# Splitting expert weights on GpSimd instead of ScalarE and VectorE in a perceiver, attention and experts kernel

## The reference, cut to what matters

```python
# x: (8, 64, 512), ctx: (8, 1601, 512), all float32
x = x + xattn(layernorm(x), ctx, ...)    # 3 rounds of slot attention with a GRU cell
x = x + attn(layernorm(x), Wqkv, bqkv, Wo, bo)   # 16 heads of 32, sequences of 64
x = x + ffn(layernorm(x), ...)

def _expert(xf, w1, w3, w2):
    return jax.nn.silu(xf @ w1) * (xf @ w3) @ w2

def ffn(x, ...):                         # 512 rows in all, D = 512, H = 256
    logits = xf @ router_w + router_b
    topk_vals, topk_idx = jax.lax.top_k(logits, 2)
    gates = softmax over the two chosen experts, 0 for the others
    routed = jax.vmap(_expert, in_axes=(None, 0, 0, 0))(xf, routed_w1, routed_w3, routed_w2)   # 8 experts
    routed_out = jnp.einsum('etd,te->td', routed, gates)
    shared_out = the same with 2 shared experts, summed
    return routed_out + shared_out
```

## Time and profile before

| what | us |
|---|---|
| median of 3 runs | 975.69 (975.63 to 976.13) |
| the profiled execution | 976.91 |
| its span in the trace | 975.2 |
| `head_attention`, from POOL's memset to its last DVE instruction | 734.99 to 813.68 |
| POOL's constants in `experts`, L1613 to L1618 | 813.96 to 815.11 |
| `experts`, shared blocks and what lies ahead of them | 813.96 to 886.03 |
| `experts`, routed blocks | 886.03 to about 953.6 |

### The profile page before, as it was taken

The page is one execution under the profiler, slowest core; times in us unless marked ns, Lnnn a source line. Parts: engine busy times, 40 slices in busy tenths (PEclk is TensorE's granted clock), DMA queues, the critical chain, the costliest instruction groups (busy, mean ns, idle before and its releaser), DMA issues. The chain is left out here.

```text
span 975.2 us, 37746 instructions
## 1 busy us (share of the span) xinstructions
PE 789.1 (81%) x17278; PEld 657.8 (67%) x17278; DVE 594.9 (61%) x1109; ACT 366.1 (38%) x714; POOL 145.8 (15%) x390
## 2 busy tenths in 40 slices
PE   3697789989889979889989797956797866786991
PEld 1445689889889979789979797856456644333440
DVE  2777456866776947857857746353425765895222
ACT  3676415324424315434335212011235523573330
POOL 3020111211313021304113111010000000130003
PEclk9799789999999999999999999987796985887996
DMA  9867970372380480843451806033349305041435
GB/s 343 320 131 133 242 144 5 52 148 96 64 228 5 68 224 4 139 154 53 58 186 31 197 4 132 5 114 103 121 87 300 100 20 180 18 130 33 128 89 161
DMA packets 178953, 115.74 MB, mean 119 GB/s; under 512 B 145196, under 2 KB 157540, under 8 KB 175596
## 3 DMA queue, kind: packets, MB, share of 16 engines
q1 hardware_dynamic: 166048, 100.45, 41.2%
q10 hardware_dynamic: 11004, 7.61, 2.6%
q0 software_dynamic: 1744, 5.27, 1.9%
HBM read 61.94 MB, written 12.85 MB: 77 GB/s over the span
## 5 line engine op out<-in xcount | busy, mean ns | idle before, releaser
L987 PE MATMUL score<-qa,ctxT 128*128 128x64 f16 x3744 | 122.6, 196 | 19.3 <-issue 11.6
L987 PEld LDWEIGHTS score<-qa,ctxT 128*128 128x128 f16 x3744 | 118.7, 100 | 21.7 <-issue 13.0
L1006 PE MATMUL score<-qa,unit 128*128 128x64 f16 (+1 forms) x2496 | 122.8, 197 | 9.9 <-issue 8.2
L1006 PEld LDWEIGHTS score<-qa,unit 128*128 128x128 f16 (+1 forms) x2496 | 121.4, 101 | 11.5 <-issue 11.3
L1006 PE MATMUL score<-scratch,unit 128*128 128x64 f16 (+1 forms) x1248 | 121.1, 197 | 3.1 <-issue 3.1
L938 PEld LDWEIGHTS gate<-hs,whhT 128*128 128x128 f16 x3456 | 112.3, 100 | 16.7 <-issue 10.7
L938 PE MATMUL gate<-hs,whhT 128*128 128x64 f16 x3456 | 114.6, 196 | 9.7 <-issue 9.2
L1006 PEld LDWEIGHTS score<-scratch,unit 128*128 128x128 f16 (+1 forms) x1248 | 114.9, 101 | 2.8 <-issue 2.8
L938 PE MATMUL gate<-qa,Bt 128*128 128x64 f16 x3456 | 105.2, 193 | 3.2 <-DVE qa L761 2.8
L938 PEld LDWEIGHTS gate<-qa,Bt 128*128 128x128 f16 x3456 | 102.6, 98 | 3.6 <-DVE qa L761 3.0
L516 ACT ACTIVATE unit<-unit,rrow 128x512 f16<-128x512 f32 x96 | 65.4, 716 | 34.3 <-POOL rrow L95 18.9
(11 more groups left out here) (254 smaller groups left out, 1343.7 us busy)
## 6 DMA issues: line engine op xcount, KB each, us to landing
unit<-in_ctx_dram SPq DMA_DIRECT2D x23, 1024.0 KB, 9.8
wall<-in_L_ffn_routed_w_dram SPq DMA_DIRECT2D x24, 512.0 KB, 8.7
xg_scratch<-wall SPq DMA_DIRECT2D x1, 3840.0 KB, 15.0
y_scratch<-ctxT ACTq DMA_DIRECT2D x15, 256.0 KB, 2.0
ctxT<-in_L_xattn_gru_wih_dram SPq DMA_DIRECT2D x3, 1024.0 KB, 17.5
ctxT<-in_L_xattn_gru_whh_dram SPq DMA_DIRECT2D x1, 3072.0 KB, 26.0
ctxT<-in_L_attn_Wqkv_dram SPq DMA_DIRECT2D x12, 256.0 KB, 8.3
ctxT<-in_L_ffn_shared_w_dram SPq DMA_DIRECT2D x6, 512.0 KB, 6.2
```

Of the source, the lines that this page charges most:

```text
L987: mm = pe.matmul(score[n][:, t * K:(t + 1) * K], a, q, start=(k == 0), stop=(k == 3 * DC - 1), skip_group_check=True)
L1006: mm = pe.matmul(score[n][:, dc * K:(dc + 1) * K], a, q, start=first, stop=True, skip_group_check=True)
```

## The change

POOL takes over the split of all 12 shared pieces and of 26 (`BY_POOL`) of the 48 routed ones. [...] The 12 shared pieces and routed pieces 0 to 13 (`IN_HEADS`) are done in `head_attention` behind the memset, routed pieces 14 to 25 in `experts` between the constants and the scatter. ACT and DVE keep pieces 26 to 47, 22 in all, spread as 2, 3, 3, 3, 2, 3, 3, 3 over the shared blocks, and lose the four big instructions for the shared weights. ACT's first piece, 26, waits until POOL has done 25 pieces, its second until it has done 26; both waits stand in ACT's list behind `tanh_of(0)`. The shared halves now lie in place in `ctxT`, so `got`, `ysb` and `gs` move to `e.room`, and two waits on the shared split go.

```diff
+BY_POOL = 26
+IN_HEADS = 14
@@ head_attention, gpsimd
             pool.memset(prob, 0.0).then_inc(zeroed, 1)
+            for n in range(NS * CHUNKS):
+                if n % CHUNKS == 0:
+                    pool.wait_ge(e_all.shared_in[n // CHUNKS], 48)
+                if n >= 2:
+                    pool.wait_ge(e_all.shared_split, n - 1)
+                split_on(pool, e_all, "shared", n, n, e_all.shared_split)
+            routed_on(pool, e_all, 0, IN_HEADS)
@@
+def halves_of(e, kind, n):
+
+    if kind == "routed":
+        span, high, low = e.wall[:], 2 * n, 2 * n + 3
+        raw = span[:, low:low + 2]
+    else:
+        span, high, low = e.free[1].bitcast(F16).rearrange("p (s d) -> p s d", d=D), max(2 * n - 1, 0), 2 * n + 2
+        raw = span[:, low:low + 2]
+    return raw.rearrange("p s d -> p (s d)").bitcast(F32), span[:, high], span[:, low]
+
+def split_on(pool, e, kind, n, count, done):
+
+    raw, high, low = halves_of(e, kind, n)
+    pool.tensor_scalar(raw, raw, WS, None, ALU.mult).then_inc(e.scaled, 1)
+    pool.wait_ge(e.scaled, count + 1)
+    pool.tensor_copy(high, raw).then_inc(e.high_made, 1)
+    pool.wait_ge(e.high_made, count + 1)
+    pool.tensor_tensor(low, raw, high, ALU.subtract).then_inc(done, 1)
+
+def routed_on(pool, e, first, end):
+
+    for n in range(first, end):
+        if n % CHUNKS == 0:
+            pool.wait_ge(e.wall_in[n // CHUNKS], 48)
+        if n >= 2:
+            pool.wait_ge(e.routed_split, n - 1)
+        split_on(pool, e, "routed", n, NS * CHUNKS + n, e.routed_split)
@@ experts
-        ws = e.room[:, 0:NS * CHUNKS * D].bitcast(F16).rearrange("p (n i c d) -> p n i c d", n=NS, i=2, c=CHUNKS)
-        got = in_1[:, 0:2 * RT * D].rearrange("p (j t d) -> p j t d", j=2, t=RT)
-        ysb = in_1[:, 2 * RT * D:3 * RT * D].rearrange("p (b d) -> p b d", b=RT)
+        got = e.room[:, 0:2 * RT * D].rearrange("p (j t d) -> p j t d", j=2, t=RT)
+        ysb = e.room[:, 2 * RT * D:3 * RT * D].rearrange("p (b d) -> p b d", b=RT)
@@
         def chunks_in(b):
-            return (min(CHUNKS * b, NW), min(CHUNKS * (b + 1), NW))
+            n = NW - BY_POOL
+            return (BY_POOL + n * b // NSB, BY_POOL + n * (b + 1) // NSB) if b < NSB else (NW, NW)
@@ experts, gpsimd
+            routed_on(pool, e, IN_HEADS, BY_POOL)
             pool.wait_ge(e.zeroed, 16)
...
-            pool.wait_ge(ws_lo, NS)
-            pool.wait_ge(ws_hi, NS)
@@ experts, scalar: shared_high(0) ahead of the router and shared_high(1) at b = 1 go
                 for n in range(first, end):
-                    if n % CHUNKS == 0:
+                    if n % CHUNKS == 0 or n == BY_POOL:
                         act.wait_ge(wall_in[n // CHUNKS], 48)
-                    if n >= 2:
-                        act.wait_ge(wall_lo, n - 1)
-                    act.activation(wall[:, 2 * n], wall_raw(n), ACT.Copy, scale=WS).then_inc(wall_hi, 1)
+                    if n < BY_POOL + 2:
+                        act.wait_ge(e.routed_split, n - 1)
+                    else:
+                        act.wait_ge(wall_lo, n - 1 - BY_POOL)
+                    raw, high, low = halves_of(e, "routed", n)
+                    act.activation(high, raw, ACT.Copy, scale=WS).then_inc(wall_hi, 1)
@@ experts, vector: shared_low(0) behind normalise and shared_low(1) behind find_places go
@@ experts, tensor
-                    pe.wait_ge(ws_hi, s + 1)
-                    pe.wait_ge(ws_lo, s + 1)
+                    if t == 0:
+                        pe.wait_ge(e.shared_split, CHUNKS * (s + 1))
                 else:
                     if k == 0:
-                        pe.wait_ge(wall_hi, NW)
-                        pe.wait_ge(wall_lo, NW)
+                        pe.wait_ge(e.routed_split, BY_POOL)
+                        pe.wait_ge(wall_hi, NW - BY_POOL)
+                        pe.wait_ge(wall_lo, NW - BY_POOL)
```

More of the change, by code:

```diff
@@ L1544, in experts @@
         th = in_0[:, 3 * RT * D:].rearrange("p (b h) -> p b h", b=2)
-        gs = in_1[:, 3 * RT * D:].bitcast(F16).rearrange("p (b i h r) -> p b i h r", b=2, i=2, h=HH)
-        spare = e.room[:, NS * CHUNKS * D:]
+        spare = e.room[:, 3 * RT * D:]
+        gs = spare[:, D:2 * D].bitcast(F16).rearrange("p (b i h r) -> p b i h r", b=2, i=2, h=HH)
         earlier = spare[:, 0:P]
@@ L1566, in experts @@
         x_ready, x_turned, x_out, x_hi, x_lo, r_in, x16_hi, x16_lo, routed, consts, picked, counted, gexp_in, gexp_out, gates_out, \
-            placed, owned, scattered, ws_hi, ws_lo, wall_hi, wall_lo, hid_done, tanhd, g_done, g_turned, gs_hi, gs_lo, \
+            placed, owned, scattered, wall_hi, wall_lo, hid_done, tanhd, g_done, g_turned, gs_hi, gs_lo, \
             down_done, shared_out, y_copied, summed, o_out, dve_done = (sem(n) for n in (
                 "x_ready", "x_turned", "x_out", "x_hi", "x_lo", "r_in", "x16_hi", "x16_lo", "routed", "consts", "picked", "counted",
-                "gexp_in", "gexp_out", "gates_out", "placed", "owned", "scattered", "ws_hi", "ws_lo", "wall_hi", "wall_lo",
+                "gexp_in", "gexp_out", "gates_out", "placed", "owned", "scattered", "wall_hi", "wall_lo",
                 "hid_done", "tanhd", "g_done", "g_turned", "gs_hi", "gs_lo", "down_done", "shared_out", "y_copied", "summed", "o_out",
@@ L1586, in wall_half, with shared_half @@
             return span[:, bass.ds(reg, 1), 2 * chunk].rearrange("p a d -> p (a d)")
+        def shared_half(s, i, chunk):
+            return halves_of(e, "shared", CHUNKS * s + chunk)[1 + i]
         def chunks_in(b):
-            return (min(CHUNKS * b, NW), min(CHUNKS * (b + 1), NW))
+            n = NW - BY_POOL
+            return (BY_POOL + n * b // NSB, BY_POOL + n * (b + 1) // NSB) if b < NSB else (NW, NW)
         block = ctx.enter_context(nc.Block())
@@ L1638, in _ @@
         def _(act):
-            def shared_high(s):
-                act.wait_ge(e.shared_in[s], 48)
-                act.activation(ws[:, s, 0].rearrange("p c d -> p (c d)"), shared_raw[s], ACT.Copy, scale=WS).then_inc(ws_hi, 1)
             def wall_high(first, end):
                 for n in range(first, end):
-                    if n % CHUNKS == 0:
+                    if n % CHUNKS == 0 or n == BY_POOL:
                         act.wait_ge(wall_in[n // CHUNKS], 48)
-                    if n >= 2:
-                        act.wait_ge(wall_lo, n - 1)
-                    act.activation(wall[:, 2 * n], wall_raw(n), ACT.Copy, scale=WS).then_inc(wall_hi, 1)
+                    if n < BY_POOL + 2:
[4 more added lines that the diff above has]
+                    act.activation(high, raw, ACT.Copy, scale=WS).then_inc(wall_hi, 1)
             def tanh_of(b):
@@ L1697, in _ @@
             st = Steps(dve, dve_done)
[L1699 to L1702, removed]
             def wall_low(first, end):
                 for n in range(first, end):
-                    dve.wait_ge(wall_hi, n + 1)
-                    dve.scalar_tensor_tensor(wall[:, 2 * n + 3], wall_raw(n), WS, wall[:, 2 * n], ALU.mult, ALU.subtract).then_inc(wall_lo, 1)
+                    dve.wait_ge(wall_hi, n + 1 - BY_POOL)
+                    raw, high, low = halves_of(e, "routed", n)
+                    dve.scalar_tensor_tensor(low, raw, WS, high, ALU.mult, ALU.subtract).then_inc(wall_lo, 1)
             def gated(b):
@@ L1786, in _ @@
             normalise(dve, st, rows, xn, e.mv, small, x_ready)
-            shared_low(0)
             dve.wait_ge(x_hi, 1)
@@ L1795, in _ @@
                     find_places()
-                    shared_low(1)
                 if b == 4:
@@ L1839, in w_half @@
                     def w_half(i):
-                        return ws[:, s, i, dc] if k < 0 else wall_half(owner_of[k], i, dc)
+                        return shared_half(s, i, dc) if k < 0 else wall_half(owner_of[k], i, dc)
                     for a, w in split_passes(x_half, w_half):
@@ L1865, in w_half @@
                     def w_half(i):
-                        return ws[:, s, i, DC + h] if k < 0 else wall_half(owner_of[k], i, DC + h)
+                        return shared_half(s, i, DC + h) if k < 0 else wall_half(owner_of[k], i, DC + h)
                     for a, w in split_passes(lambda i: gs[:, b % 2, i, h], w_half):
@@ L1946, in perceiver_kernel @@
         e.free = (words(big.ctxT[0]), words(big.ctxT[1]), in_last[:, RT * D:])
-        e.raw = [e.free[1][:, n * CHUNKS * D:(n + 1) * CHUNKS * D] for n in range(NS)]
+        e.raw = [e.free[1][:, (n * CHUNKS + 1) * D:((n + 1) * CHUNKS + 1) * D] for n in range(NS)]
         e.xg_d = nc.dram_tensor("xg_scratch", [NB * P, 2 * D], F16)
@@ L1958, in perceiver_kernel @@
         e.wall_in = [sem(f"wall_in{n}") for n in range(NE)]
+        e.scaled, e.high_made = sem("scaled"), sem("high_made")
+        e.shared_split, e.routed_split = sem("shared_split"), sem("routed_split")
         big.v_moved = sem("v_moved")
```

8 lines of the change are left out of this document (removed).

## The result

The changed kernel took 998.12 us in the median of 4 runs (996.5 to 1000.64), the kernel before 975.66 in 4 runs beside it (971.88 to 976.13). The ratio is 1.0241, with a 95% interval of 1.0207 to 1.0275. The forecast was 994.4, slower, with a range of 966 to 1006.

The account below looks back on a forecast made before the run. DVE was taken to bound the shared stage. The head stage's +16.3 and +2.4 up to the first routed block gave +18.7 us: 995.6 by the profiled execution, 994.4 us for the median, range 966 to 1006.

Parts of the forecast that it names:

- The price of a piece: POOL's multiplication, copy, subtraction and waits for one piece: 3.43 us, bounds 2.48 and 4.22.
- The head stage: In `head_attention`, POOL's 26 pieces plus 4 us lost beside DVE end the stage later: +16.3 us.
- Two of the signs: POOL's last head-stage piece some 16 us after DVE's last instruction; ACT waiting 15 to 20 us ahead of pieces 26 and 27.
- The second tanh: In `experts`, `tanh_of(1)` waits in ACT's list for POOL and starts at H + 44.2, before H + 26.8; H is the stage's start.
- 1 beside DVE: In `experts` ahead of `tanh_of(1)`, POOL loses 1 us beside DVE during its 12 pieces.
- From there to block 8: From `tanh_of(1)` to the first routed block: 32.7 us, before 45.3.
- The clock of block 8: At the first routed block, PE's first 12 matmuls run at full clock, 2.59 us and not 5.04: 2.4 less.
- The moved buffers and the removed waits: In `experts`, the other buffer for `got` and `ysb` costs nothing, and the removed waits had long been met.
- Rival 1: POOL's multiplication runs at L94's rate, a piece is 2.57 us, the head stage's end stays: -8.0 us, 967.7; 28%.
- Rival 2: Pieces are quick, but DVE's L1393 pairs wait for POOL: +5.6 in the head stage, -2.2 behind, +3.4, 979.1; 20%.
- The crossing: The whole change's effect crosses zero at about 3.1 us a piece; below 2.95 the head-stage term is gone.

Follow-up runs that it names:

- e1: The changed kernel with POOL's multiplication written with two operations (multiply, add 0.0) in place of one; 979.97 us, ratio 1.0027.
- e4: The changed kernel with only the 12 shared pieces on POOL, in the head stage, and all 48 routed pieces on ACT and DVE; 975.80 us, ratio 0.9985.
- e7: e1 with the sums of the exponentials kept in PSUM and not in SBUF; 974.72 us, ratio 0.9988 to the kernel before.
- e6: The changed kernel with only the shared pieces on POOL, moved to the projections, plus 80 POOL memsets in the head stage; 976.02 us, one execution.
- e8: e7 with the shared pieces on POOL in the projections and all 26 routed ones in the head stage; 965.52 us, ratio 0.9895.

## Why the prediction was right, step by step

- **The price of a piece: right.** 3.43 forecast, 3.37 measured undisturbed. The disputed term, the multiplication in the form of L90, went L90's way, and e1 shows that it is the form: with two operations it took 0.62, near the 0.53 that L94 gave. The 0.77 us estimated from the Trainium skill, GPSIMD Engine Reference, section 3.1 (Elementwise, side-by-side cycle accounting), fit neither this instruction (1.49) nor the copy (0.61); the measurement decides.
- **The head stage: right, +16.3 forecast, +17.4 measured.** POOL lost 6.7 us beside DVE (94.3 us for 26 pieces of 3.37) and not 4. Two of the signs came out otherwise: POOL's last piece ended 6.7 us after DVE's last instruction and not some 16, since DVE's own stage had grown by 10.7, for which the forecast had no term; and ACT waited 26.2 us ahead of pieces 26 and 27 (23.5 and 2.7), not 15 to 20. The sum was right for this kernel because POOL's stage, the longer one, hid DVE's.
- **The second tanh: mis-sized by 2.7 us.** H + 44.2 forecast, 46.9 measured. The term "1 beside DVE" in `experts` was the fault: two instructions of 2.29 us with two inputs cost POOL 2.0 and 2.1 us, 45.0 for the 12 pieces in place of 42.2.
- **From there to block 8: 32.7 forecast, 30.2 measured.** The term that was too long is the 7.3 us from `gated(2)` to the turn at 861.35, which I kept from the kernel before: here it was 4.6 (885.83 to 890.45). The difference goes with PE's clock. Before, PE had stood idle for 6.1 us ahead of this work and had a granted clock of 0.50 from 854.5 to 857.6; here it had stood for 1.0 us, and the clock was 1.00 from 886.3 to 890.6. The same two groups of matmuls, before and after:

```profile
855.02 2.77 PE L1869 MATMUL e_y<-room,ctxT 128*128 128x512 f16 x6
857.58 3.93 PE L1843 MATMUL e_hid<-room,unit 128*128 128x512 f16 x12
```

```profile
886.56 1.46 PE L1896 MATMUL e_y<-ctxT,room 128*128 128x512 f16 x6
887.86 2.75 PE L1870 MATMUL e_hid<-ctxT,unit 128*128 128x512 f16 x12
```

The last block's work took 4.6 us (902.96 to 907.53) where I had 4.4. That this error nearly cancels the one before it is luck.

- **The clock of block 8: wrong here.** I took 2.4 us off, since PE's pause would be 3 us. The pause was 3.10, and the first 12 matmuls still took 5.30, at a granted clock of 0.50 in 907.5 to 911.0, the lower of its two levels (1.2 and not 2.4 GHz). In e1, with a pause of 3.09, they ran at the full one (the rest stage is 86.94); in e7, with 3.09 too, they took 5.30 again. A pause of 3 us doesn't settle it; what does is open. This term makes most of the 3 us between 18.7 forecast and 21.9 measured in the spans.
- **The moved buffers and the removed waits: nothing,** as forecast (e4: 0.35 us).
- **Rival 1 (quick pieces, 967.7) was wrong in its second half.** e1 made the pieces quick, and the time was 979.97.
- **Rival 2 (quick pieces, DVE pays, 979.1) described e1,** its total even to 1 us, but by two errors of opposite sign. In the head stage it had +5.6 and +10.7 came: its term for the 16 instructions was right (5.3), but the other eight, which it left out, grew by 4.0, and 1.4 came on top, with a granted clock of 0.72 against 0.79. Behind the stage it had -2.2, with the clock in it, and -7.0 came: -4.8 up to block 8 and -2.2 behind it, from the clock. Against it I had rows 6, where DVE hardly suffered beside short reads of POOL; beside reads of 0.6 to 1.2 us (e1) it does. The sign from rows 8 is something else: that 128x4 instruction has one input and POOL's constants read nothing, and it took 0.90 us again in e6 but 0.17 in e1 and in the changed kernel. Why is open.

The crossing that I put at 3.1 us a piece was wrong in its sum already. With the 4 us beside DVE the first term is gone below 2.80 us and not 2.95, and at 38 us for each us of the piece the sum of +18.7 reaches zero at 2.94. The runs put it lower still, since DVE's longer stage takes over as the boundary once POOL's ends 6.7 us sooner, by estimate at about 3.1 us a piece (3.37 - 6.7 / 26): at 2.50 (e1) the kernel is at par with the one before, and not 8 us ahead. Two smaller slips change nothing: the working given for `find_places` makes 3.6 us and not 3.8 (3.7 measured, 881.25 to 884.97), and a piece of 2.48 makes rival 1 -9 and not -10.

## What to carry to other kernels

Idle time of GpSimd in a profile isn't free time: in these runs what it read from SBUF was paid by VectorE's instructions with two inputs there (and by L117, with one wide input), and in a dependent loop the stage grew by all of it (e1: 9.3 us more busy time, 10.7 us more stage). Before giving it work, look for the stretches in which VectorE reads PSUM or is idle, or put one of its inputs into PSUM, and then see that the work's end lies ahead of the stage's end and of the first wait on it in another engine's list. And measure the very form of a GpSimd instruction before pricing it, at two widths if not at its own: one written with a single operation took 2.4 times as long as the same with a second, idle one.

## What the runs showed of the hardware that was not expected

- A `tensor_scalar` of 128x512 float32 on GpSimd took 1.49 us with one operation and 0.62 with two (multiply, add 0.0), in place, same data.
- GpSimd's memsets of 0.52 us side by side with VectorE's two-input instructions delayed neither; its reading instructions raised a 0.69 us instruction of VectorE to as much as 1.53 (e1), and with its second input in PSUM it took 0.69 beside them (e7).
- After pauses of PE of 3.09 to 3.10 us the next 12 matmuls ran at either of the two clock levels: 2.76 us in e1, 5.30 in e7 and in the changed kernel.
- Small instructions were held up too, by as much as wide ones: VectorE's 128x4 ones in the projections, 0.16 us alone, had means of 0.39 to 0.54 beside GpSimd in e8.
